# Last chunk's feed-forward block as two half chunks, rows made by TensorE, final norm by halves

## The reference

```python
# x: 16 x 256 x 128, fp32
def attn(x):                       # per sequence of 256 tokens
    n = ln(x, g, b)
    W1 = gelu(n @ h1_w1 + h1_b1) @ h1_w2 + h1_b2
    W2 = gelu(n @ h2_w1 + h2_b1) @ h2_w2 + h2_b2
    t = tril(W1 @ W2.T) @ n
    t = ln(gelu(t), g, b)
    return x + gelu(ln(x + t, g, b) @ fm_w1 + fm_b1) @ fm_w2 + fm_b2
def ffn(x):                        # widths 128 -> 512 -> 512 -> 512 -> 128, ternary weights
    h = silu((x @ w1.T) * s1) * ((x @ w2.T) * s2)
    h = gelu((h @ h1_w.T) * h1_s)
    h = gelu((h @ h2_w.T) * h2_s)
    return (h @ w3.T) * s3
x = x + layernorm(attn(layernorm(x)))
x = x + layernorm(ffn(layernorm(x)))
```

## Time and profile before

| | us |
|---|---|
| median of 3 runs (376.24 to 377.04) | 376.3 |
| the profiled execution | 377.94 |
| its span | 376.1 |
| PE busy | 358.6 |
| DVE busy | 333.4 |
| ACT busy | 298.4 |
| POOL busy | 116.8 |

### The profile page before, as it was taken

One profiled execution on the slowest core, in us unless ns is written; L12 is line 12 of the kernel. 1 busy time (PEld: TensorE's weight loads), 2 busy tenths in 40 slices (PEclk: granted clock), 3 DMA queues, 4 the chain that ended last, 5 costly groups with the idle time before them and its releaser, 6 DMA issues.

```text
span 376.1 us, 5883 instructions
## 1 busy us (share of the span) xinstructions
PE 358.6 (95%) x1751; PEld 289.8 (77%) x1751; DVE 333.4 (89%) x978; ACT 298.4 (79%) x515; POOL 116.8 (31%) x186
## 2 busy tenths in 40 slices
PE   7889999989999999999999999999999999999891
PEld 6658788867888788878788878788787877778681
DVE  5899999999999987999899988888978989987735
ACT  4798899787679796998688779897798769878670
POOL 5520312641182017421832083034600352061111
PEclk9899999999999999999999999999999999999998
DMA  7761000000000000100000000000000100000001
GB/s 235 227 204 57 0 2 1 3 0 0 3 0 0 2 1 0 30 0 3 0 30 0 2 15 14 0 2 29 2 2 0 30 1 0 1 27 3 0 30 31
DMA packets 8545, 9.27 MB, mean 25 GB/s; under 512 B 576, under 2 KB 6336, under 8 KB 8512
## 3 DMA queue, kind: packets, MB, share of 16 engines
q1 hardware_dynamic: 7968, 8.60, 7.5%
q10 hardware_dynamic: 544, 0.26, 0.2%
HBM read 6.77 MB, written 2.10 MB: 24 GB/s over the span
## 4 chain that ended last, share of the span: by engine, by line
PE 84%; DVE 9%; ACT 3%; issue 2%; DMA 1%; POOL 0%; POOLq 0%; SPq 0%; DVEq 0%; ACTq 0%
PE bank L1144 9%; PE bank L1142 8%; PE bank L1177 7%; PE bank L1178 7%; PE bank L1026 6%; PE bank L1030 6%; PE bank L1045 6%; PE bank L1042 6%; PE bank L1027 5%; PE bank L1043 5%; PE bank L1069 4%; PE bank L972 4%; PE bank L1125 4%; PE bank L1128 3%; PE bank L1056 3%
## 5 line engine op out<-in xcount | busy, mean ns | idle before, releaser
L434 ACT ACTIVATE h_hidden_hi<-bank,cols 128x512 fp32r<-128x512 f32 x64 | 43.1, 706 | 14.6 <-PE bank L1030 13.4
L635 DVE TENSOR_TENSOR ffn_gate_lo<-bank,ffn_gate_hi 128x512 fp32r<-128x512 f32 x64 | 42.5, 684 | 6.4 <-ACT bank L504 5.4
L635 DVE TENSOR_TENSOR h_hidden_lo<-bank,h_hidden_hi 128x512 fp32r<-128x512 f32 x64 | 42.1, 678 | 2.9 <-ACT bank L439 2.6
L504 ACT ACTIVATE bank<-bank,cols 128x512 f32<-128x512 f32 x64 | 41.4, 671 | 0.7
L439 ACT ACTIVATE bank<-bank,cols 128x512 f32<-128x512 f32 x64 | 41.4, 679 | 0.1
L1142 PE MATMUL bank<-ffn_gate_hi,ffn_w_hi 128*128 128x512 f32 x92 | 37.3, 406 | 0.8 <-ACT ffn_gate_hi L489 0.8
L1144 PE MATMUL bank<-ffn_gate_lo,ffn_w_hi 128*128 128x512 f32 x92 | 36.3, 395 | 0.4 <-DVE ffn_gate_lo L635 0.4
L301 POOL TENSOR_SCALAR ln_f_ve<-ln_f_mv 128x4 f32<-128x4 f32 x8 | 1.8, 227 | 94.9 <-DVE ln_f_mv L625 94.9
L1026 PE MATMUL bank<-aT_hi,attn_w_lo 128*128 128x512 f32 x64 | 26.6, 415 | 0.9 <-DVE attn_w_lo L635 0.6
L498 ACT ACTIVATE ffn_gate_hi<-bank,cols 128x512 fp32r<-128x512 f32 x32 | 21.5, 697 | 7.3 <-PE bank L1144 4.6
L498 ACT ACTIVATE ffn_h_hi<-bank,cols 128x512 fp32r<-128x512 f32 x32 | 21.6, 701 | 7.1 <-PE bank L1144 4.7
(11 more groups left out here) (163 smaller groups left out, 1111.5 us busy)
## 6 DMA issues: line engine op xcount, KB each, us to landing
...
```

The lines of the kernel that those rows point to most:

```text
L434: nc.scalar.activation(dst, bank(f"{L}u{j}", c)[:, :], ACT.Gelu, bias=bias_of(L, j)).then_inc(*hi[L].done(c, j))
L635: return nc.vector.tensor_tensor(dst, whole, high.bitcast(f32), ALU.subtract)
```

## The change

The change has four parts. The two rows g and b are no longer broadcast by a DMA: PE transposes the columns g and b, spread over 128 columns, and ACT copies the result to `bc`; only the row `fm_b2` is loaded, and the columns are loaded second in the queue. The feed-forward block of chunk 7 runs as two half chunks, numbered 7 and 8, of 256 tokens each; every matmul, ACT and DVE instruction of them is 256 wide, with semaphores of their own (`HalvedSteps`). `last_product` and the two-engine evict go; each half has its `product("w3", ...)`, `w3_evict` and `f_transpose`. The final norm of the last chunk is done by halves, with the sum of variance and eps on DVE and the power on POOL. And the orders on all four engines and the bank turns are written anew for all chunks. The core of the diff, of the orders only the start and the end:

```diff
-            sp.dma_start(bc[:, :, :], rows.rearrange("(o r) d -> o r d", o=1).broadcast_to([P, 3, D])).then_inc(rows_in, 16)
+            sp.dma_start(cols[:, :], columns).then_inc(cols_in, 16)
             attn_piece(0)
-            sp.dma_start(cols[:, :], columns).then_inc(cols_in, 16)
             attn_piece(1)
             attn_piece(2)
+            sp.dma_start(b2_row[:, :], rows[2:3, :]).then_inc(b2_in, 16)
             x_piece(1, 1, 2)
...
+            def last_rstd(k):
+                pool.wait_ge(*last_ve.at(0, k))
+                half = slice(2 * k, 2 * k + 2)
+                nc.gpsimd.tensor_tensor(LN["f"]["r"][:, half], LN["f"]["ve"][:, half], neg_half[:, half], ALU.pow).then_inc(*last_r.done(0, k))
...
+            def rows_out():
+                act.wait_ge(*rows_made.at(0))
+                nc.scalar.activation(flat(bc[:, :, :]), bank("rb", 0)[:, 0:2 * P], ACT.Copy).then_inc(*rows_ready.done(0))
...
+        def span(c):
+            return slice(0, N) if c < LAST else slice(2 * P * (c - LAST), 2 * P * (c - LAST) + 2 * P)
...
-            attn_w_hi(0); attn_w_hi(1); n_high(0); nT_high(0); attn_w_hi(2); attn_w_hi(3); up_hi("h1", 0, 0); up_hi("h1", 1, 0)
+            rows_out(); attn_w_hi(0); attn_w_hi(1); attn_w_hi(2); attn_w_hi(3); attn_w_hi(4); n_high(0); attn_w_hi(5)
+            nT_high(0); ffn_w_hi(0); up_hi("h1", 0, 0); up_hi("h1", 1, 0); up_act("h1", 0, 0); up_act("h1", 1, 0); ffn_w_hi(1)
...
+            layer_hi("b", 3, 6); gate_tanh(0, 7); gate_tanh(0, 8); layer_act("b", 3, 6); gate_tanh(1, 7); gate_tanh(1, 8)
+            gate_tanh(2, 7); gate_hi(0, 7); w3_evict(6); gate_hi(1, 7); gate_tanh(3, 7); gate_hi(0, 8); gate_tanh(2, 8)
+            gate_hi(2, 7); gate_hi(3, 7); gate_hi(1, 8); gate_tanh(3, 8); gate_hi(2, 8); gate_hi(3, 8); layer_hi("a", 0, 7)
+            layer_act("a", 0, 7); layer_hi("a", 1, 7); layer_act("a", 1, 7); layer_hi("a", 2, 7); layer_act("a", 2, 7)
+            layer_hi("a", 3, 7); f_normalise(6); layer_act("a", 3, 7); layer_hi("a", 0, 8); layer_hi("a", 1, 8)
+            layer_act("a", 0, 8); layer_act("a", 1, 8); layer_hi("a", 2, 8); layer_hi("b", 0, 7); layer_act("a", 2, 8)
+            layer_act("b", 0, 7); layer_hi("b", 1, 7); layer_hi("a", 3, 8); layer_act("b", 1, 7); layer_act("a", 3, 8)
+            layer_hi("b", 2, 7); layer_hi("b", 3, 7); layer_act("b", 2, 7); layer_hi("b", 0, 8); layer_act("b", 3, 7)
+            layer_act("b", 0, 8); layer_hi("b", 1, 8); layer_hi("b", 2, 8); layer_act("b", 1, 8); layer_hi("b", 3, 8)
+            layer_act("b", 2, 8); layer_act("b", 3, 8); w3_evict(7); w3_evict(8); last_store()
...
+            def last_aggregate(k):
+                dve.wait_ge(*last_st.at(0, k))
+                for t in (2 * k, 2 * k + 1):
+                    last = nc.vector.bn_aggr(mv("f")[:, t, :], LN["f"]["st"][:, t, :])
+                last.then_inc(*last_ag.done(0, k))
+                dve.wait_ge(*last_ag.at(0, k))
+                half = slice(2 * k, 2 * k + 2)
+                nc.vector.tensor_scalar(LN["f"]["ve"][:, half], mv("f")[:, half, 1], EPS, None, ALU.add).then_inc(*last_ve.done(0, k))
...
-            x_st(0); x_ag(0); n_first(0); n_second(0); attn_w_lo(0); attn_w_lo(1); gate_constants(); nT_low(0); x_st(1)
+            x_st(0); gate_constants(); x_ag(0); n_first(0); attn_w_lo(0); attn_w_lo(1); attn_w_lo(2); n_second(0); attn_w_lo(3)
+            x_st(1); x_ag(1); nT_low(0); attn_w_lo(4); ffn_w_lo(0); attn_w_lo(5); up_lo("h1", 0, 0); up_lo("h1", 1, 0)
...
+            y_norm(7); layer_lo("b", 0, 6); layer_lo("b", 1, 6); yT_low(7); layer_lo("b", 2, 6); gate_1(0, 7); gate_1(0, 8)
+            gate_2(0, 7); layer_lo("b", 3, 6); gate_1(1, 7); gate_1(1, 8); gate_1(2, 7); gate_2(1, 7); gate_lo(0, 7)
+            gate_2(0, 8); gate_lo(1, 7); gate_1(3, 7); gate_lo(0, 8); gate_2(2, 7); gate_2(3, 7); gate_2(1, 8); gate_lo(2, 7)
+            gate_lo(3, 7); gate_lo(1, 8); gate_1(2, 8); gate_1(3, 8); gate_2(2, 8); gate_2(3, 8); gate_lo(2, 8); f_st(6)
...
+            layer_lo("b", 2, 8); layer_lo("b", 3, 8); last_stats(0); last_aggregate(0); last_stats(1); last_centre(0)
+            last_aggregate(1); last_sum(0); last_centre(1); last_sum(1)
...
-            fill("nT", 0, 26); n_transpose(0); fill("h1u0", 0, 3); up_mm("h1", 0, 0); up_mm("h1", 1, 0); up_mm("h1", 2, 0)
+            fill("rb", 0, 6); make_rows(); fill("nT", 0, 14); n_transpose(0); up_mm("h1", 0, 0); up_mm("h1", 1, 0)
...
+            up_mm("h1", 0, 1); up_mm("h1", 1, 1); lo_sum(2); scores(0, 0); scores(1, 0); up_mm("h1", 2, 1); up_mm("h1", 3, 1)
...
+                product("b", 1, 3, 6); layer_mm("b", 2, 6); y_transpose(7); layer_mm("b", 3, 6); product("w3", 0, 0, 6)
+                gate_mm("p", 0, 7); gate_mm("p", 0, 8); gate_mm("q", 0, 7); gate_mm("q", 1, 7); gate_mm("p", 1, 7)
+                gate_mm("p", 1, 8); gate_mm("p", 2, 7); product("w3", 0, 1, 6); gate_mm("p", 3, 7); product("w3", 0, 2, 6)
+                product("w3", 0, 3, 6); gate_mm("p", 2, 8); gate_mm("p", 3, 8); gate_mm("q", 0, 8); gate_mm("q", 1, 8)
+                gate_mm("q", 2, 7); gate_mm("q", 3, 7); gate_mm("q", 2, 8); gate_mm("q", 3, 8); product("a", 0, 0, 7)
+                product("a", 0, 1, 7); product("a", 1, 0, 7); product("a", 1, 1, 7); product("a", 1, 2, 7)
```

More of the change, by code:

```diff
@@ L870, in f_end, with last_centre, last_sum @@
+            def last_centre(k):
+                dve.wait_ge(*x_out.at(LAST - 1))
+                for t in (2 * k, 2 * k + 1):
+                    last = nc.vector.tensor_scalar(FN[:, t, :], last_tile(t), mv("f")[:, t, 0:1], None, ALU.subtract)
+                last.then_inc(*last_centred.done(0, k))
+            def last_sum(k):
                 dve.wait_ge(*last_shifted.at(0))
-                dve.wait_ge(*f_rstd.at(LAST, 1))
-                dve.wait_ge(*last_centred.at(0))
-                for t in range(T):
+                dve.wait_ge(*last_r.at(0, k))
+                dve.wait_ge(*last_centred.at(0, k))
+                for t in (2 * k, 2 * k + 1):
@@ L1172, in layer_mm @@
                     bank_free(g, c)
+                    dst = bank(g, c)[:, span(c)]
                     for k in range(J):
```

669 lines of the change are left out of this document (329 added, 340 removed), and 43 rows, old and new, of the table TURNS.

## The result

| | before | after |
|---|---|---|
| median, first chip | 376.27 (4 runs) | 379.0 (4 runs) |
| ratio, first chip | | 1.0065 (95% 1.0043 to 1.0088) |
| median, second chip | 376.99 (35 runs) | 377.86 (12 runs) |
| ratio, second chip | | 1.0013 (0.9992 to 1.0035) |
| the profiled execution | 377.94 | 379.03 |

The forecast was 373.7, that is 2.6 us less, in a range of 371.6 to 376.6. The change made the kernel slower: by 2.7 us on the chip of the forecast, where each side has four runs.

What follows compares the result with a forecast made beforehand. PE was taken to bound the kernel, busy 358.6 of 376.1 us, so gains come only where it idles or its clock is low. -1.4 + 0.5 - 0.8 - 0.9 = -2.6 us: median 373.7, range 371.6 to 376.6.

Steps and rivals of the forecast that it cites:

- the frame of the sum: Whole kernel: span changes counted from the profiled run (377.94 us, span 376.1) are added and applied to the median, 376.3.
- part A: Start, rows by TensorE and new order: third long matmul 1.4 us late, stalls 3.1 to 0.3 us; -1.4 us.
- part C: Last feed-forward block, chunk 7 in halves: last matmul pair ends at about 367.6, not 368.4; -0.8 us (-1.6 to +1.5).
- the last store: End of the kernel: the store keeps its 2.26 us (373.84 to 376.1), no change.
- B, middle: 31 to 342.9 us, new order and banks: one more wait on PE, +0.5 us (-2.6 to +2.6).
- D, final norm: Final norm by halves: 1.56 us saved, 0.57 given back; -0.9 us (0 to -1.6).
- Rival 1: Start: third matmul at 12.9, half clock for 16 matmuls instead of 8; +2.1 to 2.4 us, 376.0; chance 0.12.
- The stalls between 11 and 31 us: Start: 3.1 us of PE stalls from 10.93 to 30.95 us, coming from DVE, of which 0.3 are left.
- the 2 to 4 named as the test: Middle: PE idle from 60 to 340 us should be 2 to 4 us.
- rival 3: Middle: DVE blocked in chunk turns 1 to 5, 1.0 us each, +5; sum +1.9, 378.2; chance 0.12.
- The gate stage: Last block: PE waits 1.4 us for product("a", 1, 2, 7) and 0.6 for chunk 8; idle 2.05 us, before 1.3.
- The gelus' pitch: Last block on ACT: 256-wide gelus about 0.355 us each (bounds 0.29 and 0.47), against 0.577 at 512 columns.

Runs made afterwards that it cites:

- before_look2: The kernel before, unchanged, a second look with a profile: 376.35 us.
- after_again: The kernel after, unchanged, run once more: 377.86 us, ratio to before 1.0013.
- start_fills: After, with 22 instead of 14 identity transposes before chunk 0's first transposes and 16 more behind them: 376.09 us, ratio to before 0.9963.
- mixed_best: Before's orders up to chunk 6 with after's TensorE rows and end, gate_constants behind x_st(0), chunk 7's layer a gelus reordered: 376.47 us, ratio to before 0.9984.
- norm_by_halves: gate_late plus only the final norm by halves, chunk 7 left whole: 375.60 us, ratio to before 0.9961.
- gate_late: Before, with only gate_constants moved behind n_second(1) on DVE: 375.66 us, ratio to before 0.9963.
- before_look1: The kernel before, unchanged, a first look with a profile: 376.24 us.
- start_sp_waits: After, with SP issuing the first ffn load only when the last attention piece has landed: 378.28 us, ratio to before 1.0023.
- one_stream: After, without the second copy of PE's program, for weights that are not ternary: 376.83 us, ratio to before 0.9997.

## Why the prediction was wrong

Four steps failed: the frame of the sum, which took the savings from a profiled run that wasn't like the median; in part A the moment of the first long matmul and the clock behind it; in part C the size; and the last store, which the sum put at no change. The table goes from before_look2 to after, both read at the same milestones. After has two tiles of chunk 1 (six matmuls of 0.228, 1.37 us) done ahead of the scores, which is taken off.

| part | forecast | measured | from |
|---|---|---|---|
| A, start | -1.4 | +1.75 | scores 31.00 - 27.88 - 1.37 |
| B, middle | +0.5 | 0.0 | block 343.03 - 341.29, less A |
| C, last block | -0.8 | +0.3 | 25.90 - 25.58 |
| D, final norm | -0.9 | -0.97 | 4.39 - 5.36 |
| last store | 0 | +1.6 | 3.88 - 2.27 |
| sum | -2.6 | +2.7 | 377.2 - 374.5 |

**A, the frame.** "I add the changes of the span and apply them to the median" joined two kinds of run. The trace had eight matmuls at the half clock, 1.6 us, which the median run has not. So the saving was counted from a start that is 1.5 us slower than the median's (scores 29.38 against 27.88). The 1.6 us between the profiled run and the median stood in the text, and I left them alone.

**A, the size of the delay.** Expected was: last piece lands at 10.3, then one cast and `nT_high`, first matmul at 11.5. Missed was that ACT takes its casts in order: from the cast of piece 3 it has three casts, `n_high` and `nT_high` to do (one of the three stands behind `n_high`), 3.07 us from the first of them to the first matmul (10.11 to 13.18; in after_again 8.73 to 11.81, the same). What decides is when piece 3 is there, not piece 5. In after_again that gives 11.81 and a third matmul at 12.80, 0.4 us later than forecast; in the profiled run of after piece 3 came late and it was 14.17.

**A, the clock.** Rival 1 had the mechanism, PE without work between the transposes and the first long matmul, and a longer half clock (chance 0.12). It held for 8 matmuls in after and 14 in after_again, and for none in two of the four traces of before. The price of 0.2 us for each was right, and most of it reached the scores: start_fills had 2.3 us back between the third matmul and the scores, 1.6 us at the scores themselves. The forecast named "if the half clock lasts beyond 15 us" as a sign of being wrong; it lasted until 16.7 us in after and 17.9 in after_again. What I set against the rival, that "PE was at half clock before as well", is true of only a part of before's runs. The stalls between 11 and 31 us went away as forecast: PE is busy for 13.96 of 14 us from 17 to 31. So the reading of those was right, and it was paid with the clock.

**B.** The order of the middle costs nothing: scores to last block, two tiles added, is the same within 0.1 us. PE idles 1.6 us from 60 to 343 us, less than the 2 to 4 named as the test, and rival 3 isn't seen.

**C.** The gate stage came out right in sum: by the distances of starts PE stood 2.0 us between 343.03 and 351.13 us, where the forecast had 2.05. How it was made up was not foreseen, so the match is partly luck. The forecast had one wait of 1.4 us at `product("a", 1, 2, 7)` and another of 0.6 for chunk 8. The trace has 0.9 us of gap at `product("a", 1, 0, 7)`, whose bank `gate_lo(2, 7)` sets free, and the rest in short waits among the gate products. The gelus' pitch was right: 15 steps in 364.02 - 358.68 = 5.34 us, 0.356 each (forecast 0.355). By the Trainium skill (ScalarE: Activation LUTs, section What ACT_TABLE_LOAD costs) 0.40 had been the estimate; the trace speaks for the rows. That the rows agree with the page at 512 columns was true of a single gelu only (0.69 us in rows 9, 0.71 by the page); the pitch there, 0.577, was already under the page's 0.61.

What was missed is a sum of small terms. 256-wide matmuls start up to 0.1175 us apart in a run of them (16 in 1.88 us), not 0.114, which makes PE's work 22.9 us instead of 22.3. Behind the gate stage come 0.3 us of short waits, and the last products take 0.65 instead of 0.3 us, where ACT is busy without a gap, which had been named as a sign of error. Together 1.2 us. Counted in this way PE's stalls in the block are 3.0 us, in before_look2 3.2: the half chunks saved 0.2 us of stalls and cost 0.5 us of work. That ACT's order was the cause is spoken against by mixed_best. The rest of this account is read from the trace; no run changed the width alone.

**D** came as worked out: 4.39 us against a forecast of 4.5, from 5.36.

**The store.** "The store keeps its 2.26 us" failed. The trace of before had the same packet between 373 and 374 us, but its store landed after 1.9 us, and the forecast didn't look at what else moved there. In after PE's last work ends at 370.0 us, and the packet that its jump calls for moves between 374 and 375, while the store that was issued at 373.36 is under way. On this pair D's gain of 1.0 us was given back, and 0.6 more. That the shorter norm is what brings the two together is inferred: norm_by_halves alone, without the half chunks, had both stores late (2.9 and 2.8 us, where gate_late had 2.2 and 2.1), but before_look1 with the long norm had one of 2.7 as well.

So of the miss of 5.3 us 1.5 are the frame, 1.65 the start beyond it, 1.1 C and 1.6 the store, less 0.5 for B and 0.1 for D. How it splits depends on the run taken for before: from before_look1 A is +2.65, the store +0.8, and the rest the same within 0.1.

The working has small slips that change nothing: D's terms, 1.56 less 0.57, make 1.0 and not 0.9, and behind 368.4 us PE still does four transposes.

**What stays open.** Why a wait of 1.23 us is followed by the half clock in one run and not in the next. How much of the store's 1.6 us is in the median. And why after lies 0.65% over before on one chip and 0.13% on another: the share of before's runs with a half clock (14 of 35 over 377.3 us on the second, 13 of them with a low mean clock) may explain it, but on the first only four runs were made. Nor is the clock the whole account of after's spread: of its four runs on the first chip the slowest, 379.28 us, had a mean clock of 0.995, the other three 0.984 or 0.985, and two runs each of start_sp_waits (378.86 and 379.06 us, 0.995) and one_stream (377.38 and 378.30, 0.997) are like it. None of these five was profiled, so what they lost instead isn't known.
